# VectorE takes each k.k and q.k product two ticks past the product's own tick in place of one

## What is computed

```python
x = x + 0.5 * ffn(layernorm(x))
x = x + attn(layernorm(x))
x = x + 0.5 * ffn(layernorm(x))

# ffn: 256 -> 1024 -> 1024 -> 1024 -> 256, ternary weights
h = silu(x @ w1.T * w1_s) * (x @ w2.T * w2_s)
h = gelu(h @ h1.T * h1_s); h = gelu(h @ h2.T * h2_s); return h @ w3.T * w3_s

# attn: 16 heads of 16; k is normalised per head; beta = sigmoid(...)
for t in tokens:                      # lax.scan
    retrieval = S @ k_t
    S = S + outer(beta_t * (v_t - retrieval), k_t)
    o_t = S @ q_t
return x + o @ w_out + b_out
```

## Time and profile before

| | |
|---|---|
| runs | 1805.43, 1806.7, 1808.03 us; median 1806.7 us |
| profiled execution | 1805.1 us, of which the span from first to last instruction is 1803.4 us |
| busy | PE 1724.1 us (96%), VectorE 1241.3 us (69%), POOL 1208.7 us (67%), ACT 1055.8 us (59%) |
| granted TensorE clock | 0.997 of full speed |

### The profile page before, as it was taken

The page is one execution under the profiler, slowest core; times in us unless marked ns, Lnnn a source line. Parts: engine busy times, 40 slices in busy tenths (PEclk is TensorE's granted clock), DMA queues, the critical chain, the costliest instruction groups (busy, mean ns, idle before and its releaser), DMA issues.

```text
span 1803.4 us, 29772 instructions
## 1 busy us (share of the span) xinstructions
PE 1724.1 (96%) x10030; PEld 1069.7 (59%) x10030; DVE 1241.3 (69%) x2890; ACT 1055.8 (59%) x2115; POOL 1208.7 (67%) x1501
## 2 busy tenths in 40 slices
PE   6989989999999999999999999999999999999999
PEld 5865545555555555555555555588655555555588
DVE  5255777777776877868767687777776868767331
ACT  4656555565656565656556474666656555655454
POOL 4463876667676667677676767677776767675653
PEclk9999999999999999999999999999999999999999
DMA  7100000000000000000000000000000000000000
GB/s 286 49 1 1 1 1 1 1 1 1 1 1 1 24 1 24 1 1 1 1 1 1 1 24 1 1 25 1 1 1 1 1 1 13 1 1 13 1 13 13
DMA packets 5270, 23.16 MB, mean 13 GB/s; under 512 B 640, under 2 KB 1664, under 8 KB 3584
## 3 DMA queue, kind: packets, MB, share of 16 engines
q1 hardware_dynamic: 5120, 21.26, 3.2%
HBM read 17.06 MB, written 4.19 MB: 12 GB/s over the span
## 4 chain that ended last, share of the span: by engine, by line
PE 63%; POOL 10%; issue 10%; DVE 8%; ACT 7%; POOLq 0%; ACTq 0%; DVEq 0%
PE ffn_bank L1101 38%; PE ffn_bank L1084 6%; PE att_bank L1150 5%; PE att_bank L1122 4%; POOL hid_lo L584 4%; PE state_bank L1158 2%; POOL pairs_lo L621 2%; POOL pairs L613 2%; PE att_bank L1137 2%; ACT hid L700 2%; PE att_bank L1138 2%; PE att_bank L1042 2%; ACT L700 1%; DVE hid L841 1%; ACT hid_hi L676 1%
## 5 line engine op out<-in xcount | busy, mean ns | idle before, releaser
L1101 PE MATMUL ffn_bank<-hid_hi,w_sb 128*128 128x512 f16 (+1 forms) x2736 | 904.8, 346 | 8.6 <-ACT gate L687 4.6
L1101 PE MATMUL ffn_bank<-hid_lo,w_sb 128*128 128x512 f16 (+1 forms) x2736 | 904.6, 346 | 0.0
L584 POOL TENSOR_TENSOR hid_lo<-hid,hid_hi 128x512 f16<-128x512 f32 (+1 forms) x456 | 462.8, 1030 | 289.9 <-ACT hid_hi L676 289.6
L613 POOL TENSOR_TENSOR pairs<-KQ 128x32 f32<-128x32 f32 (+15 forms) x496 | 325.9, 667 | 122.8 <-DVE KQ L868 104.6
L1101 PEld LDWEIGHTS ffn_bank<-hid_hi,w_sb 128*128 128x128 fp8e4 x2736 | 275.7, 101 | 206.9 <-issue 11.7
L1101 PEld LDWEIGHTS ffn_bank<-hid_lo,w_sb 128*128 128x128 fp8e4 x2736 | 268.4, 98 | 205.4 <-issue 12.1
L621 POOL TENSOR_TENSOR pairs_lo<-pairs,pairs_hi 128x448 f16<-128x448 f32 (+15 forms) x416 | 313.2, 758 | 72.4 <-ACT pairs_hi L748 72.1
L748 ACT CAST pairs_hi<-pairs 128x448 f16<-128x448 f32 (+15 forms) x416 | 174.9, 438 | 159.7 <-POOL pairs L613 154.4
L676 ACT CAST hid_hi<-hid 128x512 f16<-128x512 f32 (+1 forms) x456 | 234.9, 552 | 31.0 <-DVE hid L841 30.4
L700 ACT ACTIVATE hid<-ffn_bank,par_sb 128x512 f32<-128x512 f32 (+1 forms) x304 | 171.6, 616 | 120.7 <-PE ffn_bank L1101 119.9
L1084 PE MATMUL ffn_bank<-xn_hi,w_sb 128*128 128x512 f16 (+1 forms) x532 | 177.4, 348 | 11.5 <-DVE hid L841 8.3
(11 more groups left out here) (92 smaller groups left out, 2134.5 us busy)
## 6 DMA issues: line engine op xcount, KB each, us to landing
NK<-in_w SPq DMA_DIRECT2D x11, 1024.0 KB, 6.0
X<-in_x SPq DMA_DIRECT2D x7, 512.0 KB, 3.4
out<-X SPq DMA_DIRECT2D x7, 512.0 KB, 2.6
wqkvb_sb<-in_wqkvb SPq DMA_DIRECT2D x1, 1024.0 KB, 9.1
X<-in_x SPq DMA_DIRECT2D x2, 256.0 KB, 6.6
out<-X SPq DMA_DIRECT2D x2, 256.0 KB, 2.1
wout_sb<-in_wout SPq DMA_DIRECT2D x1, 256.0 KB, 10.0
par_sb<-in_par SPq DMA_DIRECT2D x1, 24.0 KB, 2.4
```

The source lines that it names most:

```text
L584: pool.tensor_tensor(hid_lo[layer % 2][:, m, call.cols], hid[:, u % HID_BUFFERS, call.cols], hid_hi[layer % 2][:, m, call.cols], ALU.subtr ...
L613: pool.tensor_tensor(packed(pair(pairs, q, dot), n), later, earlier, ALU.mult).then_inc(pairs_made if dot in SPLIT else pairs_ready, 1)
L1101: mm = nc.tensor.matmul(ffn_ps(call, j), weight(name, kk, 2 * pair + i), v[:, kk, cols], start=kk == 0 and part == 0, stop=kk == KT_FF - 1 ...
```

## The change

A constant `TAKE_LAG = 2` is brought in. VectorE takes each product at the product's tick + 2 where it was + 1, and the bookkeeping that tells TensorE from which count on a bank has been read goes by the same tick. No instruction is added or removed, no tick of another engine is moved, and the three banks stay.

```diff
+TAKE_LAG = 2
 SAVE_LAG = 2
 USES, WHEN, READ_AT = [], {}, {}
@@
         for _dot in dots_at(_f, _e):
-            add_use(_dot, _f * TICKS + _e + 1, 2)
+            add_use(_dot, _f * TICKS + _e + TAKE_LAG, 2)
             WHEN[_dot] = _f * TICKS + _e
@@
                 if f >= 1 and e == E_OUT + 2:
                     add_out(f - 1)
-                for dot in dots_at(f, e - 1):
+                for dot in dots_at(f, e - TAKE_LAG):
                     if dot[0] == "qk":
                         take_qk(dot)
                     else:
                         take_kk(dot)
```

## The result

The changed kernel takes 1819.6 us (median of 4 runs, 1819.32 to 1822.11) where the kernel before takes 1806.2 us (1805.43 to 1808.03): 1.0077 times as long, with a 95% interval of 1.0065 to 1.0089, or 13.4 us more. The forecast was 1817.5 us, with 1808 to 1825 us around it. The profiled execution took 1819.6 us, its span is 1817.8 us, 14.4 us longer than that of rows 1.

The account below looks back on a forecast made before the run. TensorE's own stream was taken as the bound. Stalls of 12.0 us, less 1.9 given back, plus 0.7 travelling on, made +10.8 us: 1815.9 us in the profiled execution's terms, 1817.5 us as median, range 1808 to 1825 us.

Parts of the forecast that it names:

- The stalls at row 9: At tick 23 of frames 1 to 14, TensorE waits for row 8's take behind the residual: 12.0 us.
- the distance to the take: At tick 23 in frame 6, the moved take starts at 734.33, 0.04 us after the residual's last step ends.
- What is given back: In frames 3 and 4, mixes that hold up TensorE come earlier, now ahead of takes: together -1.9 us.
- rival C: Faster: moved takes free mixes and the turned U while stalls are partly swallowed; about 1802 us, chance 0.05.
- What travels on: Behind chunk 1's residual, VectorE's chain is 0.94 us later; later waits shrink or grow, sum +0.7 us.
- The signs: Fourteen tick-23 waits, about 12 us; q.k waits well below 88.2 us, retrieval waits up; TensorE busy within 2 us of 1724.1.
- A: TensorE's waits for POOL's low pairs swallow 8 us of the stalls: about 1809.5 us, chance 0.12.
- D: TensorE's queue hides the wait at row 9, so nothing is left: 1806.7 us, within 1 us; chance 0.05.
- B: VectorE's gapless queue costs 7.5 us more at the turned U, projection or a mix: about 1825 us, chance 0.12.

Follow-up runs that it names:

- the best version: Kernel before with q.k row 12's take at lag 3 and the spread of chunk 1's state one tick later: 1802.9 us against 1807.8, ratio 0.9974.

## Why the prediction was right

**The stalls at row 9.** Forecast 12.0 us in fourteen places, shown 10.9 us in the same fourteen: 1.33 for 1.39 us in frames 1 to 3, 0.47 for 0.52 to 0.63 us in eight frames, 1.13 for 1.26 and 1.27 us in frames 7 and 14, 0.85 for 0.98 us in frame 11. The step that was off is the distance to the take: I let it start where `terms` starts in rows 3, 0.34 us behind the start of the residual's last step, but it starts 0.21 us behind (735.85 to 736.06), since the two overlap. The matmul in turn starts 0.14 us behind the end, not 0.06. The sum is 10% too high. In frame 2, rows 5's matmul:

```profile
344.46 0.30 PE L1138 MATMUL att_bank<-pairs_hi,head_ones 128*128 128x320 f16 x1 [1.17 <-DVE qk_u L906]
```

Forecast for it was 344.55. The form in the list of waits was forecast as fourteen waits and 12 us and reads 7.7 us in 11: three more, of the 0.47 us form (frames 4, 5 and 8), are put down there to GpSimd's low pairs, and the shown ends of matmuls hide 0.16 us of each (8.6 us shown idle in all fourteen).

**What is given back.** Forecast -1.9 us in frames 3 and 4. This step failed. The rows of the changed kernel in frame 3, VectorE and then TensorE:

```profile
501.87 0.74 DVE L842 SCALAR_TENSOR_TENSOR hid<-ffn_bank,par_sb,gate 128x512 f32<-128x512 f32 x1
502.53 0.41 DVE L888 TENSOR_TENSOR qk_u<-NK,att_bank 128x256 f32<-128x256 f32 x1
...
507.66 0.44 DVE L948 STREAM_TRANSPOSE Uz<-state_bank 128x256 f32<-128x256 f32 x1
```

```profile
502.71 0.38 PE L1102 MATMUL ffn_bank<-hid_hi,w_sb 128*128 128x512 f16 x1 [1.06 <-issue]
...
508.25 0.96 PE L1159 MATMUL state_bank<-Uz,Kz 128*128 128x64 f32 x7 [0.93 <-DVE Uz L948]
```

The mix does come ahead of the take of k.k row 9, and the wait of 1.72 us in rows 10 shrinks to 1.06. But the take is now behind it, and the turned U waits for that, 0.93 us where there was no wait. Frame 4 is the same: -0.78 us at the mix, +0.79 us at the turned U. The waits for the turned U grow from 4.4 us (rows 2) to 8.9 us while those for mixes fall by 1.0 us. The prediction itself held against rival C that the backlog's sum doesn't change, and did not apply it to its own two frames. The term is about 0, not -1.9 us.

**What travels on.** Forecast +0.7 us. The kernel with row 8 alone moved shows this term unmixed. A later wait shrinks, as forecast, in frames 1, 3 and 7 (-0.62, -0.61 and -0.28 us, against -1.1 us in sum), and in frame 14 by 0.73 us, which was not. The key projections of frames 6 and 8, forecast at +0.9 us together, are not late at all; frame 15 pays 0.7 us (0.54 in the changed kernel), not 0.9. Small steps that no line of the forecast had come in frames 5, 9, 10 and 13 (1.4 us in all). Without the long norm of frame 11, the sum is about 0. In the changed kernel the largest late step lies in frame 8, at the turned U, and it is not row 8's: it stands unchanged (1.61 us) in the kernel with row 8 kept back. The key projection behind it (956.82) doesn't wait. VectorE, then TensorE:

```profile
945.00 0.74 DVE L842 SCALAR_TENSOR_TENSOR hid<-ffn_bank,par_sb,gate 128x512 f32<-128x512 f32 x1
947.70 0.75 DVE L842 SCALAR_TENSOR_TENSOR hid<-ffn_bank,par_sb,gate 128x512 f32<-128x512 f32 x1 [1.96 <-ACT gate L688]
948.37 0.55 DVE L906 TENSOR_TENSOR qk_u<-att_bank,U_sb 128x384 f32<-128x384 f32 x1
948.95 0.56 DVE L908 TENSOR_REDUCE O_in<-qk_u 128x32 f32<-128x384 f32 x1
949.42 0.44 DVE L948 STREAM_TRANSPOSE Uz<-state_bank 128x256 f32<-128x256 f32 x1
```

```profile
950.00 1.69 PE L1159 MATMUL state_bank<-Uz,Kz 128*128 128x64 f32 x8 [2.68 <-DVE Uz L948]
```

It is what moving row 11 did above: VectorE idles 1.96 us for a gate, with a ready take queued behind the waiting mix, and then does the take in front of the turned U.

**What the sum lacked.** It lacked the lower clock. The changed kernel has stretches of it at 120.8, 950.3, 1458.9 and 1544.2 us, before at 103.2, 120.2 and 263.6 us; from frame 1 on that is +3.3 us. Two errors nearly cancel: the stalls were put 1.1 us too high, and the give-back (-1.9) with what travels on (+0.7), forecast at -1.2 us together, came to -0.4 us. With the head, 10.9 + 3.3 - 0.4 + 0.6 = 14.4 us, the difference of the spans. Over the four executions the mean clock is 0.995, a loss of 9.1 us by (1 - clock) x span; before, on the four chips of the experiments, loses 4.9 to 6.4 us, so the clock has some 3 to 4 of the 13.4 us. The cause forecast is the one found; that +10.8 us came as near to +13.4 as it did owes a little to luck.

**The signs.** The waits at row 9 are there, and TensorE's matmul of pairs had never waited for VectorE before. Two of the signs were given too narrowly. TensorE's busy time rose by 3.9 us, not by up to 2 (its instructions are shown longer at the lower clock), and VectorE's waits for q.k products fell by 9 us only, while those for retrievals rose by 23 us, more than the 0.9 us a frame of the take that left its place.

**The rivals.** A (stalls swallowed behind the low pairs) has little for it: those waits went from 20.8 to 22.4 us, of which 0.9 us are the three at row 9. What did come back of the stalls came back at other waits: 2.2 us with row 8 alone moved, made up for by small late steps, and some 7 us of 25.5 with row 8 at lag 3. C and D fell. B named the mechanism that the experiments found underneath, VectorE's chain without a gap, but charged it on top of the bank's wait. Little of it adds to that: with the bank free, the take costs 11.8 us, some 9 of them in VectorE's chain; with the bank short, 13.4 us is all there is. The forecast's reasoning, "the bank is short, so TensorE waits", describes the changed kernel, but as advice (give it another bank) it would have been wrong, as the run with row 9 at tick 25 shows.

## What to carry to other kernels

In an in-order queue, ask of every moved instruction what waits in front of its new place: a ready one put behind one that waits turns idle time into lateness of everything behind it, and here 0.9 us of ready work per frame, moved past one residual, cost 13 us, while a take moved past the norm won 2.6 us. When a stall shows at a bank, test with the bank freed before believing that the bank is the cause; a second limit of nearly the same length may lie under it. A gain at one wait is only a gain if the queue behind it gets shorter, not just reordered. And before a difference of 1 or 2 us between two traces is given to an edit, look at a stretch that the edit doesn't touch, and at the granted clock of all executions.

## What the hardware showed

**The clock falls behind waits.** Several times in each kernel the granted clock of TensorE is at the lower of its two levels (1.2 of 2.4 GHz) for 3.41 us. In before and in the changed kernel each of them but the one at the very end begins within 1.2 us of the end of a wait, though the engine was busy otherwise. Windows of the kernel before around the key projection of rows 11 (start and end, length, busy us and count of PE, weight loads, VectorE, ScalarE, POOL, then granted clock, DMA share, GB/s):

```profile
260.00:263.40 3.40, 0.69 (x4) 0.10 (x1) 3.37 (x7) 1.13 (x3) 0.48 (x1) 1.00 0.00 0
263.40:267.00 3.60, 3.59 (x9) 2.69 (x10) 2.85 (x4) 0.99 (x2) 1.76 (x2) 0.53 0.00 0
```

In the kernel with row 12's take behind the norm, the wait there is 1.60 us, not 2.72, and here the clock stays up:

```profile
260.00:263.00 3.00, 1.44 (x7) 0.49 (x5) 2.96 (x7) 1.11 (x3) 1.22 (x2) 1.00 0.00 0
263.00:267.00 4.00, 3.97 (x18) 2.61 (x19) 3.93 (x6) 2.92 (x7) 1.10 (x1) 1.00 0.00 0
```

Nine instructions at the lower clock in 3.6 us, against 18 in 4.0 us: such a stretch costs up to 1.7 us (the same instructions take 1.69 us longer here). The changed kernel has the same behind the 2.68 us wait in frame 8:

```profile
946.00:950.00 4.00, 1.33 (x7) 0.47 (x6) 2.27 (x5) 3.99 (x7) 2.04 (x3) 1.00 0.01 2
950.00:953.40 3.40, 3.40 (x13) 2.24 (x14) 3.37 (x4) 0.28 (x1) 3.18 (x3) 0.54 0.02 5
```

Apart from the very end, before has three such stretches (two of them in the head), the changed kernel four (one in the head), the kernel with row 8 at lag 3 nine (one of them 6.83 us long), the best version only the two in the head.

The length of the wait alone doesn't decide. In frame 1 a projection's wait of 2.60 us is followed by a stretch in the kernel with row 8 kept back (265.5 us) and by none in the changed kernel. The wait of 3.09 us in the head is the same in all thirteen traces, and is followed by a stretch in before and five others (at 102.6 to 103.2 us) and by none in the other seven. The 2.38 us wait for a gate, at 1187.1 us in before, is also in all, and in four of them a stretch follows. And in frame 14 of the changed kernel the stretch begins while TensorE waits for row 9, after 0.9 us of idle time. So that the clock stays up because a wait got shorter is not shown, and one stretch more or less in a single trace, 1.7 us, says little about an edit.

**A VectorE norm four times as long beside POOL.** In frame 11 the norm took 0.82 us in before. In the kernel with only the sum moved it took 3.21 us, while POOL (GpSimd) went from one instruction to the next. Before, then that one (VectorE and POOL):

```profile
1248.34 0.82 DVE L828 TENSOR_TENSOR xn<-xc,roots 128x512 f32<-128x512 f32 x1
1248.57 1.61 POOL L621 TENSOR_TENSOR pairs_lo<-pairs,pairs_hi 128x512 f16<-128x512 f32 x1
```

```profile
1253.16 3.21 DVE L828 TENSOR_TENSOR xn<-xc,roots 128x512 f32<-128x512 f32 x1
1253.39 1.18 POOL L621 TENSOR_TENSOR pairs_lo<-pairs,pairs_hi 128x512 f16<-128x512 f32 x1
1254.51 1.32 POOL L584 TENSOR_TENSOR hid_lo<-hid,hid_hi 128x256 f16<-128x256 f32 x2
```

In before POOL's instruction was the one stretched (1.61 for 1.18 us), here it is VectorE's, and the key projection of frame 11 comes 1.95 us later. The same norm took about 3.2 us with row 8 kept back, with row 8 alone moved and with the k.k takes alone moved, where the 1.95 us are nearly the whole cost (2.2 us), 3.51 us with rows 11, 12 and 14 moved, and 2.75 us in the changed kernel with row 9 at tick 25.

It happens in before as well, with another norm of the same size:

```profile
1088.85 3.39 DVE L828 TENSOR_TENSOR xn<-xc,roots 128x512 f32<-128x512 f32 x1
```

POOL works there without a gap until 1091.70, and the norm ends at 1092.24. This is regular: in all thirteen traces, each such norm of over 2.4 us ends 0.54 or 0.55 us behind the end of a row of POOL's instructions that has no gap (1255.83 and 1256.37 in the rows above). So in these cases the norm's length is set by how long POOL's row goes on.

Perfetto Trace Analysis of the Trainium skill (section Optimizing Scalar/DVE Operations) says that GPSIMD and VectorE share a read port of SBUF, and that a VectorE instruction which uses two ports holds it exclusively. The rows agree in that one of the two engines is stretched where both work; that VectorE is the one that waits, and for 2.4 us, is what the rows show beyond it. No run takes the port away, so that it is the port is not shown, and what decides which of the two is stretched I did not isolate.
